# Two attention loops written out, and the projections of hyperbolic attention issued a step sooner

## The reference, cut to what matters

```python
q, k, v = (x @ w.T split into 16 heads of 8, for wq, wk, wv)
diff_sq = |q|^2 + |k|^2 - 2 q.k
denom   = max((1 - |q|^2) * (1 - |k|^2), 1e-6)
dist    = arccosh(max(1 + 2 * diff_sq / denom, 1))
attn    = softmax(-dist)            # over the 256 keys
out     = (attn @ v) @ wo.T
```

## Time and profile before

| | |
|---|---|
| median of three runs | 2562.73 us |
| the profiled execution | 2565.39 us, span 2563.6 us |
| mean granted TensorE clock | 0.844 |
| busy over the span | PE 2079.1, DVE 1998.1, ACT 1854.7, POOL 1663.5 us |
| causal attention | up to about 900 us |
| hyperbolic attention | from about 1290 to about 2430 us |

### The profile page before, as it was taken

One profiled execution on the slowest core, in us unless ns is written; L12 is line 12 of the kernel. 1 busy time (PEld: TensorE's weight loads), 2 busy tenths in 40 slices (PEclk: granted clock), 3 DMA queues, 4 the chain that ended last, 5 costly groups with the idle time before them and its releaser, 6 DMA issues. The chain is left out here.

```text
span 2563.6 us, 50172 instructions
## 1 busy us (share of the span) xinstructions
PE 2079.1 (81%) x14935; PEld 1515.9 (59%) x14935; DVE 1998.1 (78%) x6007; ACT 1854.7 (72%) x3188; POOL 1663.5 (65%) x1516
## 2 busy tenths in 40 slices
PE   4999999999999979999947666666666666666599
PEld 4777777777777668888834444443433444434266
DVE  4677777777777757877768999999999999999522
ACT  2666666666666634344239999999999999999743
POOL 2767766676667400000058999999999999999600
PEclk7999999999999969999966677777777777777599
DMA  5000000000000024334200000000000000000011
GB/s 136 1 2 2 1 1 0 1 0 1 1 0 1 2 67 108 93 92 110 68 1 1 1 1 0 0 0 0 0 0 0 0 0 0 0 0 1 7 31 37
DMA packets 44067, 49.03 MB, mean 19 GB/s; under 512 B 5112, under 2 KB 27038, under 8 KB 43934
## 3 DMA queue, kind: packets, MB, share of 16 engines
q1 hardware_dynamic: 35614, 43.32, 7.0%
q10 hardware_dynamic: 8320, 4.19, 0.7%
HBM read 42.78 MB, written 4.72 MB: 19 GB/s over the span
## 5 line engine op out<-in xcount | busy, mean ns | idle before, releaser
L1460 POOL TENSOR_TENSOR u<-u,spare 128x1024 f32<-128x1024 f32 x256 | 597.2, 2372 | 35.1 <-ACT spare L1433 34.9
L545 ACT ACTIVATE prob<-s_ps,nmax 128x128 f32<-128x128 f32 (+1 forms) x1024 | 364.4, 432 | 140.1 <-DVE nmax L602 140.0
L1353 PE MATMUL d_ps<-rowsT 28*128 28x256 f32 x1024 | 165.9, 404 | 331.3 <-DVE u L1532 331.2
L602 DVE CUSTOM_DVE_ANT_0 s_ps<-s_ps,mask 128x128 f32<-128x128 f32 (+1 forms) x1024 | 341.3, 385 | 101.8 <-issue 77.9
L1353 PEld LDWEIGHTS d_ps<-rowsT 28*128 28x128 f32 x1024 | 106.2, 242 | 430.4 <-issue 430.0
L582 POOL TENSOR_TENSOR g_lo<-g_all,g_hi 128x512 fp32r<-128x512 f32 x256 | 329.1, 1286 | 21.4
L1528 DVE TENSOR_SCALAR u<-d_ps 128x1024 f32<-128x1024 f32 x256 | 311.9, 1218 | 39.5 <-PE i_ps L1353 39.3
L1532 DVE SCALAR_TENSOR_TENSOR u<-i_ps,u 128x1024 f32<-128x1024 f32 x256 | 313.5, 1225 | 14.8
L1471 POOL TENSOR_TENSOR spare<-spare,u 128x1024 f32<-128x1024 f32 x128 | 303.1, 2368 | 10.7
L1447 ACT ACTIVATE u<-u 128x1024 f32<-128x1024 f32 x256 | 258.3, 1070 | 0.0
L1450 ACT ACTIVATE u<-u 128x1024 f32<-128x1024 f32 x256 | 257.5, 1066 | 0.0
(11 more groups left out here) (265 smaller groups left out, 5577.9 us busy)
## 6 DMA issues: line engine op xcount, KB each, us to landing
w_all<-w_rows SPq DMA_DIRECT2D x128, 256.0 KB, 5.6
x<-L_attn_x ACTq DMA_DIRECT2D x8, 512.0 KB, 14.0
y<-y_rows SPq DMA_DIRECT2D x16, 256.0 KB, 2.3
wkqv<-L_attn_Wkqv SPq DMA_DIRECT2D x4, 528.0 KB, 8.7
gate_rows<-L_ffn_gate_proj SPq DMA_DIRECT2D x1, 512.0 KB, 14.5
up_rows<-L_ffn_up_proj SPq DMA_DIRECT2D x1, 512.0 KB, 11.5
down_cols<-L_ffn_down_proj SPq DMA_DIRECT2D x1, 512.0 KB, 13.3
w_rows<-wT SPq DMA_DIRECT2D x8, 64.0 KB, 1.6
```

The lines of the kernel that those rows point to most:

```text
L545: last = nc.scalar.activation(prob[:, kind, at, :].rearrange("p c n -> p (c n)"), s_ps[kind][:, at.start * P:at.stop * P], ACT.Exp, bias=n ...
L602: last = nc.vector.tensor_tensor_reduce(out=scores, in0=scores, in1=keep.mask[:, N - width:N], scale=-1.0, scalar=3.4e38, op0=ALU.add, op1 ...
L1353: last = nc.tensor.matmul(ps[:, e * W2 + j * N:e * W2 + (j + 1) * N], rowsT[at, slot(i, p), 1, j * P:(j + 1) * P], rowsT[at, slot(i, p), 0 ...
L1460: nc.gpsimd.tensor_tensor(u[:, slot(i, p), :], u[:, slot(i, p), :], spare[:, p % SPARE, :], ALU.add).then_inc(sum_done, 1)
```

## The change: what it does

Both loops become straight code. In `dve_max` the memset of the spare column goes, in `pool_product` the four-element add. In hyperbolic attention the following moves:

| work | before | after |
|---|---|---|
| turn of the tokens of a batch, and its copy | step 0 of the batch before | step 7 (copy: after the roots of pair 6) of the batch two before |
| projection of blocks 0 and 1 | steps 1 and 2 | steps 0 (behind row turns 5, 6) and 1 (behind row turn 7) |
| hi 0 on ScalarE | behind the first four of the weights | between their logarithms and exponentials |
| lo 0 on VectorE | step 2 | step 1, ahead of the distances of pair 2 |
| second half of the features | step 4 | step 5, ahead of normalisation 0 |
| turning back of block 1 | step 5, behind the values and row turn 0 | step 5, ahead of the values |
| last projection on TensorE | step 7, ahead of row turn 4 | step 7, behind it, and waits for the copy of turned tokens |

```diff
-            nc.vector.memset(nmax[:, kind, GH:GH + 1], 0.0)
...
-        def over_turns(engine, body):
...
+        def over_pairs_of_batches(body):
+            for p in range(pairs):
+                body(p, p % 2, p == 0, p == pairs - 1)
...
         def pe_turn_x(pe, b):
             pe.wait_ge(xh_done, (b + 1) * TB)
-            after(pe, res_done, b - 3)
+            after(pe, attnT_done, b - 3)
...
         def pe_qkv(pe, b, j):
             pe.wait_ge(xT_done, b + 1)
+            after(pe, res_done, b - 3)
...
-            nc.gpsimd.tensor_tensor(extra[:, 0:4], pair[:, 0:4], twos[:, :], ALU.add)
-            nc.gpsimd.tensor_scalar(extra[:, 4:2 * W2], pair[:, 4:2 * W2], 1.0, 2.0, ALU.mult, ALU.add).then_inc(raised, 1)
+            nc.gpsimd.tensor_scalar(extra, pair, 1.0, 2.0, ALU.mult, ALU.add).then_inc(raised, 1)
...
+        def over_batches(body):
+            for b in range(batches):
+                body(b, b % TURN, b >= 1, b >= 2, b >= 3, b + 1 < batches, b + 2 < batches)
...
-                        if one_after and p == 0:
-                            pe_turn_x(pe, b + 1)
-                        if one_after and p == 1:
-                            pe_qkv(pe, b + 1, 0)
+                        if b == 0 and p == 0:
+                            pe_turn_x(pe, 1)
                         for r in {0: (5, 6), 1: (7,)}.get(p, ()):
                             pe_turn_rows(pe, b, r)
+                        if one_after and p == 0:
+                            pe_qkv(pe, b + 1, 0)
+                        if two_before and p == BACK_AT + 1:
+                            pe_turn_o(pe, b - 2, 1, (i - 2) % TURN, b + 2 if one_after else batches)
                         if one_before and p in VALUES_AT:
                             pe_values(pe, b - 1, VALUES_AT.index(p), (i - 1) % TURN)
+                        if two_after and p == PROJECT_AT:
+                            pe_turn_x(pe, b + 2)
                         if one_after:
-                            if p == 2:
+                            if p == 1:
                                 pe_qkv(pe, b + 1, 1)
...
+                        if two_before and p == PROJECT_AT:
+                            pe.wait_ge(xT_done, b + 3 if two_after else batches)
+                            pe_project(pe, b - 2)
...
-                            if p in (2, 4):
-                                dve_lo(dve, b + 1, p // 2 - 1, (i + 1) % TURN)
+                            if p in (1, 4):
+                                dve_lo(dve, b + 1, p // 4, (i + 1) % TURN)
                             if p == 4:
                                 dve_features(dve, b + 1)
+                            if p == 5:
                                 dve_features_end(dve, b + 1)
```

More of the change, by code:

```diff
@@ L382, in causal_attention @@
         g_lo = m.sb("g_lo", [P, 2, GH, W2], F32R)
-        nmax = m.sb("nmax", [P, 3, GH + 1])
+        nmax = m.sb("nmax", [P, 3, GH])
         prob = m.sb("prob", [P, 3, 4, P])
@@ L699, in body @@
                                 pe_make_values(pe, p + 1)
-                over_turns(pe, body)
+                over_pairs_of_batches(body)
                 for s in range(SLOTS - TURN_LAG, SLOTS):
@@ L735, in body @@
                                 act_values(act, p + 1, 1 - i)
-                over_turns(act, body)
+                over_pairs_of_batches(body)
                 nc.scalar.preload_act_table_set("sqrt_and_others")
@@ L760, in body @@
                                 pool_split_x(pool, p + 1, 1 - i)
-                over_turns(pool, body)
+                over_pairs_of_batches(body)
             @block.vector
@@ L797, in body @@
                             dve_norm(dve, p + 1)
-                over_turns(dve, body)
+                over_pairs_of_batches(body)
                 for s in range(SLOTS - TURN_LAG, SLOTS):
@@ L1613, in body @@
                         if two_before:
-                            if BACK_AT <= p < BACK_AT + TB:
-                                pe_turn_o(pe, b - 2, p - BACK_AT, (i - 2) % TURN, b + 2 if one_after else batches)
+                            if p == BACK_AT:
+                                pe_turn_o(pe, b - 2, 0, (i - 2) % TURN, b + 2 if one_after else batches)
                             if p == ATTN_AT:
                                 pe_turn_attn(pe, b - 2)
-                            if p == PROJECT_AT:
-                                pe_project(pe, b - 2)
                         if one_after:
@@ L1644, in _, with weights @@
                 copy_rows(act, 0, ROWS_BY_SCALAR[0], 0)
-                def weights(b, i, p):
+                def weights(b, i, p, between=None):
                     for logarithm in (True, False):
@@ L1649, in weights @@
                             act_weights(act, b, p + n, i, logarithm)
+                        if logarithm and between is not None:
+                            act_hi(act, between, 0)
                 def body(b, i, one_before, two_before, three_before, one_after, two_after):
@@ L1654, in body @@
                         nc.scalar.preload_act_table_set("natural_log_exp_and_others")
-                    if one_after:
-                        act_xT(act, b + 1)
+                    if b == 0:
+                        act_xT(act, 1)
                     for p in range(0, HP, 2):
                         if one_before:
-                            weights(b - 1, (i - 1) % TURN, p)
-                        if one_after and p in (0, 2):
-                            act_hi(act, b + 1, p // 2)
+                            weights(b - 1, (i - 1) % TURN, p, b + 1 if one_after and p == 0 else None)
+                        elif p == 0:
+                            act_hi(act, b + 1, 0)
+                        if one_after and p == 2:
+                            act_hi(act, b + 1, 1)
                         if two_after and p == 4:
@@ L1669, in body @@
                             copy_rows(act, b + 1, ROWS_BY_SCALAR[0], (i + 1) % TURN)
-                over_batches(act, body)
+                        if two_after and p == 6:
+                            act_xT(act, b + 2)
+                over_batches(body)
                 nc.scalar.preload_act_table_set("natural_log_exp_and_others")
@@ L1693, in body @@
                         pool_sum(pool, b, p, i)
-                over_batches(pool, body)
+                over_batches(body)
             @block.vector
```

7 lines of the change are left out of this document (2 added, 5 removed).

## The result

The changed kernel takes 2601.27 us (median of four runs, 2599.30 to 2604.80), the kernel before beside it 2563.09: a ratio of 1.0148, 95% interval 1.0131 to 1.0166. It is slower, by 38 us; 2598 was forecast. The profiled execution took 2604.8 us, span 2603.0.

A forecast was written before the change was run, and what follows sets the result against it. TensorE bounds causal attention, a VectorE-TensorE ring the hyperbolic stage. +1.30 us a batch over 29 batches (37.7), 3.7 for batches 0 and 1, less causal 6.0: +35.4, so 2600.8 profiled, 2598 median; range 2554 to 2618.

The forecast's parts named there:

- the ring: Hyperbolic stage: ratio, pair matmuls, distances, ratio close between VectorE and TensorE alone; VectorE's work about 32.0 us, pauses 2.1.
- rival C: Hyperbolic stage: ScalarE was the bound and its 0.84 us wait goes; 33.28 us a batch, total 2530; chance 0.12.
- Lo 0's pause: VectorE ahead of pair 2's distances: lo 0 waits for ratio 1, row turn 7 and hi 0; +1.5 us a batch.
- Distances 3: VectorE at pair 3: with lo 0 gone from ahead, the distances wait 0.26 to 0.56 us; 0.45 taken.
- Output copy and distances 7: Block 1's turn back waits for normalisation 0, with values 3, row turn 0 and pair 7 queued behind; +1.15 us a batch.
- 0.52 and 1.18: VectorE's pauses ahead of pair 6's distances and block 1's normalisation were to vanish: -0.52 and -1.18 us a batch.
- Hyperbolic loop written out: Hyperbolic stage as straight code, from batch 30's 34.04 us against 34.15 looped: -0.1 us a batch.
- The late last projection: TensorE's final projection waits for the copy of turned tokens: 0, up to 0.3 us if ScalarE is late.
- Sum: Hyperbolic stage: all terms together +1.30 us a batch, period 35.4 from 34.15; batches 0 and 1 +1.85 each.
- Causal gain: Causal attention: twelve looped pairs at 51.70 us become straight code at 51.20, a gain of 6.0 us.
- Rival B: Hyperbolic stage: TensorE's clock rhythm absorbs VectorE's pauses, period stays, causal gain alone gives 2557; chance 0.12.

The follow-up runs named there:

- Lo at 2: Changed kernel with lo 0 on VectorE and projection 1 on TensorE back in step 2; 2555.21 us.
- two row buffers: Changed kernel, order kept, with two buffers for the feature rows so hi 0 need not wait for row turn 7 of the batch before; 2561.62 us.
- Turn behind: Changed kernel with the turn back of block 1 again behind values 3 and row turn 0, features still ended in step 5; 2558.68 us.
- two-buffer variant with repeated turns: Changed kernel with two feature-row buffers, last projection between row turns 3 and 4, and block 0's turn back issued four times; 2554.64 us.
- Loops only: Kernel before with both loops written out and nothing moved; 2556.41 us.
- two repeats: Kernel before and changed kernel, each run again unchanged, ten runs each: before 2561.45 to 2596.05 us (profiled run 2561.45), changed 2599.89 us.
- lo at 2 with turn behind: Changed kernel with lo 0 and projection 1 back in step 2 and block 1's turn back behind values 3 and row turn 0; 2550.68 us.

## Why the prediction was right

- *VectorE and TensorE close the ring; ScalarE follows.* Shown. VectorE's work is unchanged and the period follows its pauses. ScalarE's wait ahead of hi 0 grew, as forecast; rival C, which had it vanish, fell. One reading was off: "VectorE's work of about 32.0 us" is the period less the three bracketed pauses; its busy time is 93.66 / 3 = 31.22, and the other 0.8 us are gaps too short for a bracket.
- *Lo 0's pause, forecast 1.5 (1.30 to 1.76):* 1.17 in the trace. The order of events was as worked out; pair matmuls and row turn 7 ran at full clock and hi 0 to lo 0 took 0.97 instead of 1.07. The fast end was itself 0.1 too high. Lo at 2 and two row buffers confirm the chain. At 1.17 this term lay below its own range.
- *Distances 3, forecast 0.45:* 0.40.
- *Output copy and distances 7, forecast 1.15 (0 to 1.32):* 0.29 + 0.84 = 1.13. TensorE idled 2.74 us ahead of pair 6, not some 4, and still ran values 3 at half clock. Turn behind confirms that the waiting turn makes the pause; the two batches of the two-buffer variant with repeated turns show that the half clock gives it its length.
- *Gone: 0.52 and 1.18.* Both.
- *Hyperbolic loop written out, forecast -0.1:* nothing. Loops only has 34.14 for 34.15; the 34.04 of batch 30, which the term was read from, is that of a batch next to the end.
- *The late last projection, forecast 0, up to 0.3:* missed. The residual waits 0.58 in the batch shown and column 0 grew by 0.44. TensorE's row turns 3 and 4 ran at half clock (eight transposes in 1.91 us), so the projection behind them was late. The pause ahead of distances 4, which had no term, is 0.60; before it was 0.40 in one batch of three and about 0.52 in the others, so column 3 grew by 0.11.
- *Sum:* forecast +1.30 a batch, measured +1.49 in the mean of batches 3 to 28. Batches 0 and 1, forecast +1.85 each, grew by 1.27 and 0.73. Over the 31 periods the stage grew by 1103.40 - 1055.18 = 48.2 us (forecast 41.4). About 2 us of the excess lie in batch 30, which took 37.64 us, with a copy of the moments of 2.29 us in it.
- *Causal gain, forecast 6.0:* 8.95 up to the start of the hyperbolic stage. Straight pairs beside a loop took 51.20 us, straight pairs throughout 51.10; twelve looped pairs thus gave 7.2; the rest arose outside them. Why a looped pair costs 0.6 us more was not tested.

So +48.2 - 8.95 = +39.3 us of span, of 39.4 measured. That 2598 came within 4 us is in part luck: the errors of two terms, 6.8 us more loss and 3 us more gain, partly cancelled. The traces of the two repeats also show how far single executions scatter: there the stage grew by 44.3 us and its first ratio came 10.7 us sooner.

**Rival B** holds more than I gave it. Seven kernels, the one before among them, have periods of 34.14 to 34.18, though single pauses differ between them by up to 1.2 us a batch. Most of it is explained. The new order saves 0.52 + 1.18 = 1.70 us, which pays for one of its two losses: turn behind keeps lo 0's pause of 1.17, lo at 2 keeps those of 0.29 and 0.63 around pair 7, and both are back at the old period. Only the two together cost. In the variants with lo 0 back in step 2, the slower copy of the last section takes back 0.3 to 0.6 us a batch. That TensorE's clock levels matter is shown by the two-buffer variant with repeated turns: the turn and values 3 at full clock were worth 1.55 us in column 6. That they pull these seven to one period is not shown, and the mean clock does not do it: it was 0.60 in one batch of loops only and 0.72 in one of lo at 2. Two row buffers, 0.45 us under its expected period because pauses elsewhere shrank too, stays open.

## What to carry to other kernels

Where two engines hand work back and forth, the small operations between the hand-overs are cover: moving one forward is free only if all that it waits for, through every engine, is done by then, and whatever stands behind a waiting instruction in its queue is part of the price. A wait on the busiest engine (ScalarE's 0.84) may belong to the ring that it follows, so find who sets the period before trying to remove it. Redundant matmuls in an idle stretch can pay if they reach up to the work that matters: 25 us here in one order, 9 in the other. And one term undone at a time is not a sum: here either loss alone was paid for by what the new order saved.

## What the runs showed of the hardware

A copy of 128x4 numbers on VectorE takes 0.16 us when GpSimd is idle or almost done, and otherwise ends when GpSimd's running instruction ends. It first looks like an effect of the loop. By shape in the kernel before, written-out and looped:

```profile
L1566 DVE COPY mv<-part_mv 128x4 f32<-128x4 f32 x5 | 5.3, 1055 | 0.1
L1566 DVE COPY mv<-part_mv 128x4 f32 x27 | 4.3, 160 | 0.0
```

But two of those five, 1.59 and 3.19 us in the last microseconds of the stage, make the mean of 1.06. The two written-out copies in the steady batches took 0.16 like the looped ones, and so did 28 of 32 with loops only and 29 of 32 in the changed kernel. In lo at 2 with turn behind, the mean of 32 and the copy shown above beside GpSimd:

```profile
L1555 DVE COPY mv<-part_mv 128x4 f32<-128x4 f32 x32 | 25.3, 791 | 0.1
```

```profile
1932.87 2.37 POOL L1460 TENSOR_TENSOR spare<-spare,u 128x1024 f32<-128x1024 f32 x1
```

GpSimd's multiplication runs from 1932.87 to 1935.24, the copy from 1934.02 to 1935.26. Over the 14 traces 148 such copies took more than 0.2 us; each started while a GpSimd instruction ran, and each ended at most 0.03 us after one. In the changed kernel the copy fell into an idle time of GpSimd in 29 of 32 batches, so it is no part of the loss in the steady batches. In the three variants with lo 0 back in step 2 it met GpSimd in most batches: its means over batches 3 to 28 are 0.51, 0.45 and 0.75 us, and column 5 is longer by what they exceed 0.16 (4.78, 4.73 and 5.03 for 4.44).

The Trainium skill (SBUF — State Buffer, Who interferes with whom) says that a VectorE copy can enter a mode that takes the port pair shared with GpSimd, and that whoever comes second is blocked for the whole instruction of the other. The 148 copies agree with that. No run here shows whether a copy in a looped batch would be blocked too, since GpSimd was idle at all 27 of them.

TensorE's values took 1.07 us at a granted clock of 1.0 and 1.93 at 0.5, and in the old order 20 cheap transposes ahead of them decided which.
